# Turning the expert tiles between a tile's two experts, six early tiles and a split row store, in an attention and mixture-of-experts layer on one core

## What is computed

```python
x = _rmsnorm(src + sa, norm1_w)
shared = _swiglu(flat @ W_shared_in) @ W_shared_out
# a group of 4 experts is chosen, then 2 of its experts; w holds their two weights for each token
topv, topi = jax.lax.top_k(p_expert, TOPK)
h = _swiglu(flat @ W1_shared)
for e in range(E):
    routed = routed + h @ W2_experts[e] * w[:, e:e + 1]
out = x + (shared + routed).reshape(Bb, Tt, C)
return _rmsnorm(out, norm2_w)
```

## Time and profile before

| | us |
|---|---|
| median of three runs | 1475.52 (1473.75 to 1480.91) |
| the profiled execution | 1474.44 |
| its span in the trace | 1472.7 |
| expert tiles, from the first transpose (1287.0) to the last scatter (1461.01) | 174.0 |

### The profile page before, as it was taken

How to read it: one execution, slowest core, us unless ns; L and a number is a source line. 1 busy time by engine, 2 the same in 40 slices (tenths; PEclk the granted TensorE clock), 3 DMA queues, 4 the chain that set the end, 5 groups by cost and what they waited for, 6 DMA issues and landing times. The chain is left out here.

```text
span 1472.7 us, 26917 instructions
## 1 busy us (share of the span) xinstructions
PE 1381.2 (94%) x9749; PEld 816.9 (55%) x9749; DVE 1135.8 (77%) x1803; ACT 854.7 (58%) x1573; POOL 368.7 (25%) x366
## 2 busy tenths in 40 slices
PE   6999899979999999999999999989999999889995
PEld 3655576734333333333333333336888888678884
DVE  3786575598999999999999999824677777556664
ACT  2445443305888888888888888884334433223332
POOL 0343294044241000000000000101233433345553
PEclk9999999957999999999999999999999999999998
DMA  5799769252443334443343324115665544465551
GB/s 187 265 321 342 244 226 246 67 96 72 82 111 67 46 56 67 65 67 67 59 67 58 55 50 69 53 58 84 163 168 152 155 125 115 116 198 169 177 175 53
DMA packets 115362, 184.54 MB, mean 125 GB/s; under 512 B 26454, under 2 KB 65770, under 8 KB 115238
## 3 DMA queue, kind: packets, MB, share of 16 engines
q1 hardware_dynamic: 90117, 124.55, 34.2%
q0 software_dynamic: 14656, 44.66, 10.6%
q10 hardware_dynamic: 10464, 13.64, 3.0%
HBM read 101.84 MB, written 81.88 MB: 125 GB/s over the span
## 5 line engine op out<-in xcount | busy, mean ns | idle before, releaser
L1799 DVE TENSOR_REDUCE i_saT<-h_banks 128x2 f32<-128x1024 f32 x512 | 617.7, 1221 | 25.1 <-PE h_banks L1668 17.2
L1768 ACT ACTIVATE h_p<-h_banks 128x512 f32<-128x512 f32 x1024 | 551.0, 599 | 137.5 <-PE h_banks L1687 122.2
L1708 PE MATMUL h_po<-h_p,h_v 128*32 128x256 f32 (+1 forms) x3728 | 318.4, 413 | 3.5 <-ACT h_p L1768 1.3
L1687 PE MATMUL h_banks<-h_q,h_k 50*128 50x512 f32 x1024 | 254.4, 495 | 11.6 <-ACT h_p L1768 6.0
L1668 PE MATMUL h_banks<-h_k,h_q 48*128 48x512 f32 x1024 | 222.8, 431 | 10.7 <-DVE i_saT L1799 6.8
L1687 PEld LDWEIGHTS h_banks<-h_q,h_k 50*128 50x128 f32 x1024 | 95.7, 183 | 235.0 <-ACT h_p L1768 190.4
L1708 PEld LDWEIGHTS h_po<-h_p,h_v 128*32 128x32 f32 x3728 | 73.4, 108 | 170.6 <-issue 83.0
L2077 PE MATMUL f_ob<-w_experts,f_h 128*128 x1032 | 134.2, 286 | 11.7 <-issue 9.9
L2077 PEld LDWEIGHTS f_ob<-w_experts,f_h 128*128 128x128 f32 x1032 | 125.6, 190 | 21.0 <-issue 20.9
L1564 POOL COPY h_v<-h_values 128x512 f32<-128x512 f32 x14 | 8.6, 612 | 460.5 <-DMA h_values<-vh_d 420.6
L1668 PEld LDWEIGHTS h_banks<-h_k,h_q 48*128 48x128 f32 x1024 | 101.1, 194 | 38.4 <-DVE i_saT L1799 28.0
(11 more groups left out here) (266 smaller groups left out, 1699.6 us busy)
## 6 DMA issues: line engine op xcount, KB each, us to landing
h_q<-q_d SPq DMA_DIRECT2D x84, 128.0 KB, 5.8
h_k<-k_d SPq DMA_DIRECT2D x84, 128.0 KB, 6.9
ot_d<-h_o ACTq DMA_DIRECT2D x32, 256.0 KB, 2.6
q_d<-t_parts SPq DMA_DIRECT2D x12, 512.0 KB, 5.0
k_d<-t_parts SPq DMA_DIRECT2D x12, 512.0 KB, 5.2
rows_d<-h_place SPq DMA_DIRECT2D x4, 1056.0 KB, 4.2
rows_d<-f_rows SPq DMA_DIRECT2D x4, 1056.0 KB, 4.2
p_xin<-in_L_attn_x SPq DMA_DIRECT2D x8, 512.0 KB, 5.0
```

The lines of the kernel that those rows point to most:

```text
L1687: ins = nc.tensor.matmul(bank_of(key, g), k6[r][at, p, j * P:(j + 1) * P], q6[r][at, p, c * CH:(c + 1) * CH], start=True, stop=True)
L1708: ins = nc.tensor.matmul(po[h * VW:(h + 1) * VW, at], vh[n % RING][:, j, h, :], probs[u % PR][:, h, at], start=j == 0 and (part == 0 or la ...
L1768: nc.scalar.activation(probs[u % PR][:, h, :], bank_of(("PAIR", f // SIDES), f % SIDES), ACT.Exp, scale=DH ** -0.5).then_inc(exp_done, 1)
L1799: nc.vector.tensor_reduce(halfmax[n % 2][:, m, :], both_banks(("SLOT", slot)), AX.X, ALU.max)\
```

## The change

On PE the transposes of tile t + 2 and the loads of the expert numbers of tile t + 1 now stand between the two experts of tile t. The first six tiles are early ones: the two buffers `whole` are the new places, and POOL waits for its own last `low_parts` before it fills them. `store_rest` is split: the last 272 numbers of a row are stored as soon as the weights are there (the copy has moved to part 5 of the chunk, semaphore `weighed`), the 256 of the base in `store_base` when all four banks have been added. The lists are turned into a pair buffer, behind the first 36 matmuls of `shared` of the last chunk.

```diff
-        early = [flat(a)[:, i * HID:(i + 1) * HID] for a in (x1T, x1) for i in range(2)]
+        early = [flat(a)[:, i * HID:(i + 1) * HID] for a in (x1T, x1) for i in range(2)] + whole
...
             for c in range(NCH):
                 for f in range(PARTS_OF_CHUNK):
                     yield f, c
+            yield "LISTS", 0
...
-                pool.wait_ge(*banks.released(("LISTS", 0)))
+                pool.wait_ge(*fills.released(("LISTS", 0)))
...
                 for t in range(EARLY):
+                    if early[t] is whole[0]:
+                        pool.wait_ge(h_split, NCH * KH)
                     gather_early(t)
+                pool.wait_ge(rest_stored, NCH * 16)
                 pool.wait_ge(rows_stored, NCH * 16)
...
                 def load_ya(c):
                     if c >= 2:
-                        wait.ge(rows_stored, (c - 1) * 16)
+                        wait.ge(rest_stored, (c - 1) * 16)
...
                 def store_rest(c):
-                    wait.ge(summed, c + 1)
+                    wait.ge(weighed, c + 1)
...
-                    sp.dma_start(tokens(rows_d, c)[:, :, BASE:ROW], rows[c % 2][:, :, BASE:ROW])\
+                    sp.dma_start(tokens(rows_d, c)[:, :, REST:ROW], rows[c % 2][:, :, REST:ROW]).then_inc(rest_stored, 16)
+
+                def store_base(c):
+                    for j in range(TPC):
+                        wait.ge(*banks.released(("OUT", c, j)))
+                    sp.dma_start(tokens(rows_d, c)[:, :, BASE:REST], rows[c % 2][:, :, BASE:REST])\
                         .then_inc(rows_stored, 16)
...
+                        if pieces.start == 0 and c == LASTS:
+                            routing.turn_lists(pe, fills)
...
-                def experts(t):
+                def pick(i, t):
+                    return pe.value_load(picks[0:1, i, t:t + 1], min_val=0, max_val=E - 1)
+
+                def expert(t, i, e):
                     key = ("SUM", t)
-                    both = [pe.value_load(picks[0:1, i, t:t + 1], min_val=0, max_val=E - 1) for i in range(2)]
-                    pe.wait_ge(*banks.emptied(key))
-                    pe.wait_ge(*fills.released(("TILE", t)))
...
                 turn_tile(0)
+                turn_tile(1)
+                both = [pick(i, 0) for i in range(2)]
                 for t in range(TILES):
+                    expert(t, 0, both[0])
+                    if t + 2 < TILES:
+                        turn_tile(t + 2)
+                    second = both[1]
                     if t + 1 < TILES:
-                        turn_tile(t + 1)
-                    experts(t)
+                        both = [pick(i, t + 1) for i in range(2)]
+                    expert(t, 1, second)
...
                         if f == TURN_AT:
+                            if c >= 2:
+                                dve.wait_ge(rest_stored, (c - 1) * 16)
+                            nc.vector.tensor_copy(rows[c % 2][:, :, SHARES:ROW], routing.shares[c % 2])\
+                                .then_inc(weighed, 1)
...
-                    nc.vector.tensor_copy(rows[c % 2][:, :, SHARES:ROW], routing.shares[c % 2]).then_inc(summed, 1)
```

More of the change, by code:

```diff
@@ L1888, in feed_forward @@
         hidden_stored = sems("f_hidden_stored")
+        rest_stored = sem("f_rest_stored")
         rows_stored = sem("f_rows_stored")
@@ L1894, in feed_forward @@
         sil_done = sems("f_sil_done")
-        summed = sem("f_summed")
+        weighed = sem("f_weighed")
         early_in = sems("f_early_in", EARLY)
@@ L1926, in banks_order @@
                     yield "GATE", c + 1
-                else:
-                    yield "LISTS", 0
                 for j in range(TPC):
@@ L2050, in _ @@
                     store_rest(c)
+                    store_base(c)
                 for s in range(SLOTS):
@@ L2105, in turn_tile @@
                     ins.then_inc(fills.made, 1)
-                def experts(t):
+                def pick(i, t):
+                    return pe.value_load(picks[0:1, i, t:t + 1], min_val=0, max_val=E - 1)
+                def expert(t, i, e):
                     key = ("SUM", t)
-                    both = [pe.value_load(picks[0:1, i, t:t + 1], min_val=0, max_val=E - 1) for i in range(2)]
-                    pe.wait_ge(*banks.emptied(key))
-                    pe.wait_ge(*fills.released(("TILE", t)))
[L2112 to L2116, removed]
+                    if i == 0:
+                        pe.wait_ge(*banks.emptied(key))
+                        pe.wait_ge(*fills.released(("TILE", t)))
+                    ins = output(banks.buffer(key)[:, 0, i * D:(i + 1) * D],
+                                 lambda part, k: h[part][:, t % KH, k * P:(k + 1) * P],
+                                 lambda part, k: w2s[part][:, bass.ds(e, 1), k, :])
+                    if i == 1:
+                        ins.then_inc(banks.made, 1)
                 for c in range(NCH):
@@ L2127, in _ @@
                             routing.turn_tokens(pe, c + 1, banks, normal(c + 1))
-                        if f == LISTS_AT and not more:
-                            routing.turn_lists(pe, banks)
                         if f == GATES_AT and more:
@@ L2291, in _ @@
                         if f == LISTS_AT and not more:
-                            routing.take_lists(dve, banks)
+                            routing.take_lists(dve, fills)
                     if more:
```

## The result

| | median us | runs | ratio to before, 95% interval |
|---|---|---|---|
| before | 1475.53 | 20, 1472.30 to 1480.91 | |
| after | 1479.88 | 20, 1474.46 to 1491.87 | 1.0033 [1.0018, 1.0048] |

The ratio says that the change makes the kernel slower by 0.33%, 4.9 us (the two medians of the table differ by 4.4). That is less than the 0.5% that the prediction called no change, but more than nothing. The forecast was 1477.2, with a range of 1461 to 1484: 1.7 slower than before, the sum of -4.1 and +5.8. So the time lies in the range, and the loss is more than twice the one forecast.

A forecast was written before the change was run, and what follows sets the result against it. A loop of rows through POOL was taken to bound the kernel. From 1474.44 for the profiled execution, -4.1 (start) and +5.8 (steady tiles) gave 1476.1; the runs' median lies 1.1 higher, so 1477.2, range 1461 to 1484.

The forecast's parts named there:

- What bounds the kernel: Steady expert tiles: a loop of rows through POOL, not PE, sets the pace, 3.77 us a tile against 3.81 measured.
- Where it closes: Steady tiles: a turn of 15.1 us over four tiles becomes 11.7 over three, 3.91 us a tile.
- Rival D: Steady tiles: both orders share what holds the loop, POOL the nearest; only the start counts, 1471.4; chance 0.10.
- DVE's wait for ACT ahead of its rest: Sign in the steady tiles of the profile after: this wait gone, a wait of DVE's sums for PE in its place.
- What a turn has above its plain sum: Steady tiles: a surplus of 0.16 a turn, now shared by three tiles, adds 0.01 to 0.03 us a tile.
- each late landing is paid in full by three tiles: Dear end of the steady-tile loss: 0.25 us a tile, 8.5 us.
- The start: Start of the tiles: first row gather moves from 1292.48 to 1288.4, -4.1 us, with POOL, not the store, late next.
- The base store: Start of the tiles: half-size store issued at 1282.3, landing within at most 4.2 us, at 1286.5, before POOL is there.
- rival C: Slower: slow clock at the early rows leaves 2 of the 4.1, loop at 0.25 a tile, 1482.0; chance 0.16.
- DVE and ACT: Steady tiles: they don't stop the loop, busy 2.61 and 1.29 a tile; their turn let PE run at 3.26.
- B: Rival, steady tiles: number loads are hidden, PE at 3.26 a tile, -18.7 us, with the start 1452.7; chance 0.04.
- A: Rival, steady tiles: rows come in time, 3.52 a tile, -9.9 us, with the start -14, 1461.5; chance 0.14.

The follow-up runs named there:

- experiments 3 to 6: Ring of gathered rows one tile deeper: changed kernel 1462.93 (3), kernel before 1468.66 (4); one tile shallower: kernel before 1543.74 (5), changed kernel 1576.02 (6).
- experiment 2: The order alone: the kernel before with nothing but the new order on PE; 1487.04 against 1477.24, ratio 1.0076.
- the start alone: The changed kernel with the old order on PE (six early tiles, split store, later lists kept); 1474.34 against 1477.24, ratio 0.9976.
- experiments 8 and 9: 8: changed kernel, seven rows ahead, numbers of tile 0 loaded once for all tiles, 1460.27; 9: the same with rounding ahead of the root on ACT, 1450.62.
- experiments 12 and 9: 12: changed kernel, seven rows ahead, rounding ahead of the root on ACT, all number loads, 1462.56; 9: the same with tile 0's numbers loaded once, 1450.62.

## Why the prediction was right where it was, and where not

**What bounds the kernel: right.** The loop from number load over sums, scatter, gather and landing sets the pace; one row more or less in flight moves both kernels as the division says (experiments 3 to 6).

**Where it closes: right, and the turn to 0.1.** 11.7 was forecast, a quiet turn took 11.76. Rival D (both orders share what holds the loop) is out with experiment 2. DVE's wait for ACT ahead of its rest, 36.8 over the stretch before, did not vanish as I wrote, but fell to 30.3; the new wait of the sums for PE is there, 13.5.

**What a turn has above its plain sum: mis-sized.** This is the term of 0.01 to 0.03 a tile in "I take 0.17". After against the start alone is 1.0033 / 0.9976, +8.4 us or 0.25 a tile over 34 (if all of it lies there), the end of my range that I had called "each late landing is paid in full by three tiles". The order alone against before is +11.2, 0.33. I had shared out the surplus of before over fewer tiles and taken it as constant. In the one trace of the order alone it nearly was: one row landed late (5.2), and a tile took 3.96.

In the trace of after it was not, and that execution is 7.0 above the median. Six of the 37 row gathers behind the first six took 5.1 to 6.0 there instead of 4.3; before has three such (5.2, 5.2, 5.4). The 34 tiles are 7.3 above 3.91 each, and two stretches hold all of that. Between the transposes at 1354.14 and 1389.53 it is 4.1, with late rows (5.1, 5.8) and the two drops of the clock, each of which makes the next sums and gather late. Between 1416.81 and 1455.67 it is 3.7, with three late rows (5.1, 5.6, 6.0) and a granted clock of 1.00 throughout, although PE stood longer there (1.40 and 0.83 around 1434, 1.66 and 0.73 around 1448) than ahead of the first drop (0.84 and 0.83). So late rows go with all of the surplus, the slow clock with about half of it. Why a row lands late now and then, whether the new order makes that more frequent, and what the executions near the median lose stays open.

**The start: right in sum, wrong in two terms that cancelled or were covered.** The first row gather came where forecast, and the start gave -3.5 for -4.1. The base store landed 4.9 behind its issue and let POOL go on after 5.6, not at most 4.2 (what the 0.7 between are isn't shown; before they were 0.3). Six early gathers covered that by 0.3: luck, since the bound was read from a store that had the DMA engines for itself. And rival C's slow clock at the early rows did occur (0.50, first experts in 2.92) yet didn't eat the gain, since before had paid more: some 14 us at half clock between 1276 and 1320, in its 48 shared matmuls (8.69 for 5.90) and behind the fifth tile's row. The start alone has some 10 there (also behind its seventh tile's row, where 24 matmuls take 4.68), after some 7.

**DVE and ACT: a wrong reason.** I excluded them since PE had once run at 3.26 a tile. Their turn is 3.47 (experiments 8 and 9). It lies under both kernels' pace, so the sum was untouched, but B (3.26 for all tiles) could not have come true even with the loads hidden: taking them away gave 3.46. A few tiles at 3.26 with operands prepared ahead are no proof that the others can follow for long.

**The rivals.** A (rows in time) is not what happened; made to happen by a seventh row it is real, -14 us, where the prediction had -14 too. That the sums agree is luck: the steady tiles gave 7.7 for its 9.9 (3.58 a tile for 3.52), the rest of the stage 7.0 for its 4.1. The runs don't bear that out: even with rows in time the two loads and their address operations cost 0.12 a tile over the next floor, and 0.34 (3.59 against 3.25, experiments 12 and 9) when nothing else binds. C's slower side is half of what came: its loop at 0.25 a tile, not its lost start.

## What to carry to other kernels

When an instruction that waits for a transfer is moved ahead in a queue, count the tiles over which its loop closes before and after: half a tile earlier on PE was worth one whole row in flight less, and the cure was one more row ahead, not another order. A surplus over the plain sum of a loop isn't a constant that fewer tiles share: here it differed between executions, with the number of late landings and, in half of it, with a drop of the clock behind them. An engine pair's limit is read from its chain of waits in series, not from a few fast tiles that ate what had been prepared.

## What the hardware showed that I had not expected

- A store of 256 numbers a row for 512 rows, beside early gathers, took 5.6 us until POOL could gather; the store of twice that size, alone on the DMA engines, took 4.5 (1288.02 to 1292.48). A larger transfer is no bound for a smaller one that runs in other company.
- 24 matmuls ahead of 3.6 us with only eight transposes in them did nothing for the matmuls behind it: 2.92 for 12, as without them.
- Two stands of PE of 0.84 and 0.83 were followed by 3.4 us at 1.2 GHz; 1.66 and 0.73, later in the same trace, were not.
- Whole stages that an edit doesn't touch moved by some 4 us between profiled executions (the low part at 1274.30 and 1278.67 for the same code ahead of it), as much as the effect under study. Distances from a common point inside the trace told the parts of a change apart where the ends did not.
